# Delta-rule recurrence in chunks of 64 tokens, two pairs of sequences half a step apart, and mixed terms stored by whole heads

## What is computed

```python
q, k, v = (_short_conv(x @ W.T, conv) for W, conv in ...)      # 4 taps, silu
beta = sigmoid(x @ Wb.T)
# delta rule, chunk by chunk (the reference takes 32 tokens; any chunk gives the same result)
def step(S, inp):
    q_i, k_i, u_i, w_i = inp
    attn = jnp.where(causal, q_i @ jnp.swapaxes(k_i, -1, -2), 0.0)
    u_adj = u_i - w_i @ S
    o_i = q_i @ S + attn @ u_adj
    return (S + jnp.swapaxes(k_i, -1, -2) @ u_adj, o_i)
# u = T @ v, w = T @ (beta k), T the inverse of the chunk's unit lower triangle
o = p0 * fir3(v) + p1 * fir15(v) + p2 * fir63(v) + p3 * delta_out + p4 * v   # p: gates, softmax
x = layernorm(x + rmsnorm(o) @ Wo.T)
h = silu(x @ w1) * (x @ w2);  h = gelu(h @ h1);  h = gelu(h @ h2)
x = layernorm(x + h @ w3)
```

## Time and profile before

| what | before |
|---|---|
| median of 3 runs | 2404.92 us (2404.31 to 2409.49) |
| the profiled execution | 2403.26 us, span 2401.5 us |
| busy, of the span | PE 2159.4 us (90%), DVE 1209.4 (50%), ACT 926.3 (39%), POOL 521.5 (22%) |
| `delta` stage, first load to the next stage's first | 574.8 to 1067.1 us |
| one 128-token step in it | 28.0 us |
| DMA packets | 244243, of them 174162 under 512 B |
| mean granted TensorE clock | 0.962 of full speed |

### The profile page before, as it was taken

How to read it: one execution, slowest core, us unless ns; L and a number is a source line. 1 busy time by engine, 2 the same in 40 slices (tenths; PEclk the granted TensorE clock), 3 DMA queues, 4 the chain that set the end, 5 groups by cost and what they waited for, 6 DMA issues and landing times.

```text
span 2401.5 us, 40269 instructions
## 1 busy us (share of the span) xinstructions
PE 2159.4 (90%) x15412; PEld 1855.9 (77%) x15412; DVE 1209.4 (50%) x1877; ACT 926.3 (39%) x1556; POOL 521.5 (22%) x450
## 2 busy tenths in 40 slices
PE   7888864777899999949999999999999999999998
PEld 5776754666788888837888888888888888888886
DVE  6777759945676777742323432343244323323432
ACT  4554432011344444414433443444344434443442
POOL 1113787866344443410000000000000000000000
PEclk9999987788999999979999999999999999999999
DMA  3666667887899898823000000000000000000000
GB/s 125 195 196 180 198 180 216 265 291 217 210 244 249 237 243 225 221 102 160 1 18 18 17 0 17 17 17 0 17 17 16 2 17 17 0 17 17 18 1 18
DMA packets 244243, 253.36 MB, mean 106 GB/s; under 512 B 174162, under 2 KB 207442, under 8 KB 233810
## 3 DMA queue, kind: packets, MB, share of 16 engines
q1 hardware_dynamic: 231890, 210.54, 30.8%
q10 hardware_dynamic: 12288, 41.95, 5.3%
HBM read 156.77 MB, written 95.68 MB: 105 GB/s over the span
## 4 chain that ended last, share of the span: by engine, by line
PE 53%; issue 1%; DVE 1%; ACT 0%; DMA 0%; SPq 0%; POOL 0%; DVEq 0%; ACTq 0%; POOLq 0%
PE B L1671 47%; PE O L1699 5%; PE T L1627 1%; DVE yb L1798 0%; ACT gate L1737 0%; DMA wr<-wr_s 0%; SPq L1560 0%; DVE stats L1829 0%; ACT L1737 0%; DVE z L1824 0%; DVE z L1820 0%; DVE z L1843 0%; POOL rstd L1879 0%; SPq L1574 0%; DVEq L1793 0%
## 5 line engine op out<-in xcount | busy, mean ns | idle before, releaser
L1751 ACT ACTIVATE yb<-B,scol 128x512 f32<-128x512 f32 x256 | 176.2, 688 | 581.0 <-PE B L1671 581.0
L1671 PE MATMUL B<-act1l,wr 128*128 128x512 f32 x1024 | 398.4, 389 | 0.0
L1671 PE MATMUL B<-act0h,wr 128*128 128x512 f32 x1024 | 398.3, 389 | 0.0
L1671 PE MATMUL B<-act1h,wr 128*128 128x512 f32 x1024 | 398.3, 389 | 0.0
L1671 PE MATMUL B<-act0l,wr 128*128 128x512 f32 x1024 | 398.3, 389 | 0.0
L1786 DVE TENSOR_TENSOR act0l<-yb,act0h 128x512 fp32r<-128x512 f32 x256 | 176.0, 688 | 377.9 <-ACT act0h L1754 375.7
L1876 POOL TENSOR_TENSOR rstd<-mv,ln_eps 128x4 f32<-128x4 f32 x16 | 3.2, 199 | 1308.9 <-DVE mv L1837 1308.9
L441 DVE SCALAR_TENSOR_TENSOR acc<-proj,taps,acc 128x512 f32<-128x512 f32 x288 | 214.3, 750 | 85.2 <-ACT acc L387 76.7
L1786 DVE TENSOR_TENSOR act1l<-yb,act1h 128x512 fp32r<-128x512 f32 x128 | 88.6, 692 | 295.5 <-ACT act1h L1754 295.5
L1671 PEld LDWEIGHTS B<-act1l,wr 128*128 128x128 f32 x1024 | 192.2, 188 | 39.9
L1671 PEld LDWEIGHTS B<-act0l,wr 128*128 128x128 f32 x1024 | 192.2, 188 | 39.9
(11 more groups left out here) (179 smaller groups left out, 3448.7 us busy)
## 6 DMA issues: line engine op xcount, KB each, us to landing
qk_s<-yT SPq DMA_DIRECT2D x16, 1024.0 KB, 6.2
kk_s<-kfull SPq DMA_DIRECT2D x16, 1024.0 KB, 6.4
qk<-qk_s SPq DMA_DIRECT2D x16, 1024.0 KB, 6.6
lt<-kk_s SPq DMA_DIRECT2D x15, 1024.0 KB, 5.2
wraw<-in_ffn_w ACTq DMA_DIRECT2D x16, 704.0 KB, 5.9
wr_s<-wround ACTq DMA_DIRECT2D x16, 704.0 KB, 9.4
toe<-in_toe_short ACTq DMA_DIRECT2D x32, 320.0 KB, 7.2
xt<-in_xt SPq DMA_DIRECT2D x16, 524.0 KB, 4.3
```

Of the source, the lines that this page charges most:

```text
L1671: last = nc.tensor.matmul(B[slot % 4][:, :], w, part, start=(k == 0 and i == 0), stop=(k == kts - 1 and i == len(parts) - 1))
L1751: last = nc.scalar.activation(dst, B[slot % 4][:, :], ACT.Gelu, scale=scol[:, slot:slot + 1])
```

## The change

`weights_fir` keeps `mixed` for a whole head (64 features, two buffers), stores 4 times 2 MB instead of 8 times 1 MB, and `mix_s` is laid out by whole heads. `pwT` moves into memory of `raw`. The order of matrices in `kfull` and in the tables goes by sequence.

`delta` is written anew. Its unit is a group v of 32: one pair of sequences (e = v % 2) in one 128-token stretch (t = v // 2). Iteration u of 33 works the first 64 tokens of group u on partitions 0 to 63 and the second 64 tokens of group u-1 on partitions 64 to 127. So both pairs of sequences are in each iteration, and the four 32 x 32 inverses are joined only to two 64 x 64 ones (rounds "first" and "second" instead of N, A, B, C). Matmuls are on 64 x 64 quarters of the array, or on 128 x 64 halves, except the turn and the output projection. Loads have four buffers (`RING`), and one load of a kind serves half of what it did.

```diff
-C_ID, C_ATT, C_SEL, C_END = 0, P, 2 * P, 2 * P + 2
+C_ID, C_ATT, C_SEL, C_END = 0, P, P + P // 2, P + P // 2 + 2
+HC = 2 * CH
+GB = BATCH // 2
+GK = GB * KT
+GS = 2 * GK
+GROUPS = 2 * STEPS
+RING = 4
+WCH = W_END // GROUPS
 (weights_fir)
-        mixed = [st.sb(f"mixed{i}", [P, WIN, DK // 2]) for i in range(2)]
+        mixed = [st.sb(f"mixed{i}", [P, WIN, DK]) for i in range(2)]
-                    sp.wait_ge(mixed_done, (u + 1) * HALF)
+                    sp.wait_ge(mixed_done, (h + 1) * NG)
-                    if n > HALF // 2 and n % (HALF // PER_TOE) == 2:
-                        store(n // (HALF // PER_TOE) - 1)
+                    if h and g == 2:
+                        store(h - 1)
 (delta, tiles)
+        XY = st.ps("XY", [P, GK, 2, DK])
+        XO = st.ps("XO", [P, GK, 2, DK])
+        SI = st.ps("SI", [P, 2, 512])
+        Q = st.ps("Q", [P, 2, 512])
+        NA = st.ps("NA", [P, 2, GS, CH])
+        TW = st.ps("TW", [P, 512])
 (delta, SP: ten loads, two or four more, x, one store)
+                def group_in(v, r, n):
+                    sp.dma_start(qk[r][:, :, :], ...).then_inc(prep_in[p], 16)
+                    sp.dma_start(ktok[r][:, :, :], ...).then_inc(prep_in[p], 16)
+                    mats = bass.ds(t * NS + e * GS, GS)
+                    for c in range(2):
+                        j, i = FIRST[c], SECOND[c]
+                        sp.dma_start(lt[p][j, :, CH:HC], io["kk_s"][j, mats, i])
+                        sp.dma_start(tt[r][j, :, 0:CH], io["t_s"][mats, 2 * c].rearrange("s i j -> i s j"))
+                        sp.dma_start(tt[r][i, :, CH:HC], io["t_s"][mats, 2 * c + 1].rearrange("s i j -> i s j"))
+                        sp.dma_start(first_inv[p][j, :, :], io["d_s"][mats, 2 * c].rearrange("s i j -> i s j"))
+                def slot_in(part, r, p, t, e):
+                    rows = slice(part * HC, part * HC + HC)
+                    sp.dma_start(vtok[r][rows, :, :, :], ...)
+                    sp.dma_start(mix[r][rows, :, :, :],
+                                 io["mix_s"][part, bass.ds(t, 1), e * GB:(e + 1) * GB, :, :, :].rearrange("o b h m d -> m (o b) h d"))
+                def step(u, r, n):
+                    sp.wait_ge(s_ready, u + 1)
+                    sp.wait_ge(mixed, u)
+                    sp.wait_ge(prep_done, u + 2)
...
+                        group_in(u + 3, (r + 3) % RING, n + 2 if r % 2 else n + 1)
+                        slot_in(0, (r + 3) % RING, (r + 3) % 2, n + 2 if r % 2 else n + 1, (r + 3) % 2)
+                        slot_in(1, (r + 3) % RING, (r + 3) % 2, n + 1, r % 2)
+                        sp.wait_ge(res_done, u + 1)
+                        x_load(u - 1, (r - 1) % RING, n if r % 2 else n - 1)
+                        store(u - 3, (r + 1) % RING, n - 1 if r % 2 else n - 2)
 (delta, PE)
+                def from_state(u, r):
+                    pe.wait_ge(state_done, u)
+                    pe.wait_ge(u_done, u)
+                    for k in range(GK):
+                        for g, half, rows in chunks(u, r):
+                            last = nc.tensor.matmul(XY[rows, k, :, :], qk[g][:, KT + k % KT, tokens(k, half)], S[:, g % 2, k, :, :],
+                def queries_keys(v, r, n):
+                    for k in range(GK):
+                        for half in range(2):
+                            for par in range(2):
...
+                def first_round(v, r):
+                    for c in range(GS):
+                        for rows in HALVES:
+                            last = nc.tensor.matmul(NA[rows, 0, c, :], lt[r % 2][rows, c, :], first_inv[r % 2][rows, c, :],
+                def solve(u, r):
+                    pe.wait_ge(x_done, u + 1)
+                    for k in range(GK):
+                        for par in range(2):
+                            for g, half, rows in chunks(u, r):
+                                last = nc.tensor.matmul(XY[rows, k, par, :], tt[g][rows, par * GK + k, :], x0[rows, k, par, :],
+                def turn(u, r):
+                    pe.wait_ge(on_done, u + 1)
+                    pe.wait_ge(res_done, u + 2)
+                    for k in range(GK):
+                        last = nc.tensor.transpose(turned[:, k, :], o[r % 2][:, k, :, :].rearrange("p r d -> p (r d)"), ident)
+                def step(u, r, n):
+                    from_state(u, r)
+                    queries_keys(u + 1, ...)
+                    first_round(u + 1, ...)
+                    solve(u, r)
+                    queries_state(u, r)
+                    turn(u - 1, ...)
+                    new_state(u, r, n)
+                    queries_solution(u, r)
+                    second_round(u + 1, ...)
+                    project_out(u - 2, ...)
 (delta, ACT)
+                def step(u, r, n):
+                    first_out(u + 1, ...)
+                    solution(u, r)
+                    turned_out(u - 1, ...)
+                    second_out(u + 1, ...)
+                    squares(u, r)
+                    round_weights(u, r, n)
+                    raw_weights(u + 1, ...)
 (delta, DVE)
+                def step(u, r, n):
+                    right_side(u, r)
+                    head_norm(u - 1, ...)
+                    residual(u - 3, ...)
+                    causal(u + 1, ...)
+                    spread(u - 3, ...)
+                    state_out(u)
+                    outputs(u, r)
+                    compare_weights(u - 1, ...)
+                    head_sums(u)
+                    layer_norm(u - 3, ...)
 (delta, POOL)
+                def step(u, r, n):
+                    prep(u + 1, ...)
+                    tail(u - 3, ...)
+                    norm(u, ...)
-    "mix_s": (2, STEPS, BATCH, 2 * HEADS, WIN, DK // 2),
+    "mix_s": (2, STEPS, BATCH, HEADS, WIN, DK),
```

More of the change, by code:

```diff
@@ new lines, in delta, with rows_of, steps @@
+        NPREP = 10
+        LAST = GROUPS
+        def rows_of(u):
+            return slice(0, HC) if isinstance(u, int) and u == 0 else slice(HC, P) if isinstance(u, int) and u == LAST else slice(0, P)
+        def steps(engine, step, first, end):
+            loops = (end - first) // RING
+            with engine.Fori(0, loops) as i:
+                for j in range(RING):
+                    step(i * RING + (first + j), (first + j) % RING, i * (RING // 2) + (first + j) // 2)
+            return first + loops * RING
@@ L1008, in _ @@
+                for v in range(GROUPS - 3, GROUPS):
+                    store(v, v % RING, v // 2)
                 sp.wait_ge(flag_done, 1)
@@ new lines, in _ @@
+                queries_keys(0, 0, 0)
+                first_round(0, 0)
+                second_round(0, 0)
+                pe.wait_ge(ready, 4)
+                for u in range(3):
+                    if u == 2:
+                        pe.wait_ge(wo_done, 1)
+                    step(u, u % RING, u // 2)
+                u = steps(pe, step, 3, GROUPS)
+                while u <= LAST:
+                    step(u, u % RING, u // 2)
+                    u += 1
+                turn(LAST, LAST % RING)
@@ new lines, in _ @@
+                last.then_inc(tables_done, 1)
+                raw_weights(0, 0)
+                raw_weights(1, 1)
+                act.wait_ge(ready, 2)
+                first_out(0, 0)
+                second_out(0, 0)
+                for u in range(3):
+                    step(u, u % RING, u // 2)
+                u = steps(act, step, 3, GROUPS)
+                while u <= LAST:
+                    step(u, u % RING, u // 2)
+                    u += 1
+                turned_out(LAST, LAST % RING)
```

947 lines of the change are left out of this document (416 added, 531 removed).

## The result

The kernel after the change ran at 2367.05, 2370.82, 2372.29 and 2375.07 us, median 2371.56; the kernel before, beside it, at 2405.22. The ratio is 0.9856, with a 95% interval of 0.9835 to 0.9876. The change gains 33.7 us where the forecast expected 98. The profiled execution took 2375.07 us, its span 2373.2.

A forecast was written before the change was run, and what follows sets the result against it. The prediction took PE's queue to bound the kernel, with transfers not far behind. Replacing old `delta` and filter time by 24 + 32 x 11.2 - 3 + 20 gave 1949 + 32P = 2307 us, range 2272 to 2355.

The forecast's parts named there:

- The sum's form: Whole kernel: old time less old `delta` and 3 us of filters, plus beginning, 32 periods and end: 1949 + 32P.
- Filters: `weights_fir`: 6 us gained from POOL's vanished wait, 3 us lost on the 2 MB last store; net -3, between -9 and +4.
- PE's groups: `delta` loop: PE's matmul groups, transposes, projection and changes of array division take 10.7 us per iteration.
- the loop through the norms: `delta`: dependency loop from comparison through POOL's power, head norm, residual, statistics and state to outputs, 10.1 us together.
- row tiles don't queue: `solve`, `queries_solution`: alternating row tiles share a PSUM bank without queueing; the queueing rival gave P = 12.8, 2359 us, chance 0.03.
- DVE has room: `delta` loop: DVE needs 9.7 us per iteration including waits, leaving 1 us to spare.
- the period: `delta`: time per loop iteration, 11.2 us from PE's 10.7 and half a us of loss; ends 10.2 and 12.5.
- 16 x 0.68 = 10.9 us, or 16 x 0.56 = 9.0: `delta` loop: SP's time for its 16 transfer issues per iteration, the lower figure if nothing stalls.
- Transfers or SP bound the loop: Rival for the `delta` loop: P = 12 to 13.8, say 12.5, giving 2349 us, with PE idle before `queries_keys`; chance 0.13.
- In-order queues so close together don't interlock without loss: `delta` loop: reason for adding half a us of loss to PE's 10.7; PE lost 8% of a step before.
- what is late next are the Toeplitz loads: `weights_fir`: PE waits for these loads once POOL's wait goes, so 6 us of gain was counted, where 8.4 reached DVE.
- The wrong-if line: `delta` loop: the forecast is wrong if PE idles over 1 us per iteration, as the period is then not PE's.

The follow-up runs named there:

- e13: e4 with the two inverse rounds in PE's loop doing one of eight matrices, the rest left out (720 pairs in the body): 2292.28 us, one run, period 10.34.
- e1: Kernel after the change with PE's loop written out as 29 iterations, no jump back: 2366.91 us, ratio 0.9840.
- e4: Kernel after the change with the two loads of mixed terms issued by ACT instead of SP, which keeps 14 issues: 2354.84 us, ratio 0.9775.
- e6: e4 with PE's loop also written out: 2327.54 us, ratio 0.9664.
- e8: Kernel after the change with each head's mixed terms in the FIR stage stored as two 1 MB transfers instead of one of 2 MB: 2361.85 us, ratio 0.9824.
- e11: Kernel before the change with only PE's loop altered: four steps in its body instead of two, three times round: 2441.77 us, ratio 1.0148.
- e18: Against e15: PE's loop of four iterations kept, state and key products merged into larger matmuls (816 pairs in the body): 2373.25 us, ratio 0.9866.
- e15: Kernel after the change plus PE's loop written out, four loads issued by ACT, residual waiting for the store four groups ago, 1 MB FIR stores: 2308.53 us, ratio 0.9601.
- e17: Kernel after the change, all 16 issues on SP, inverse rounds in PE's loop doing one of eight matrices, the rest left out: 2346.68 us, ratio 0.9755.

## Why the prediction was wrong, point by point

- **The sum's form** held. Loop 413.8 us against 32 x 11.2 - 3 = 355.4, +58.4. First solve 20.6 us into the stage, forecast 24: -3.4. From the last one to `ffn` 23.8, forecast 20: +3.8. Filters +6.3, forecast -3: +9.3. Together +68.1, and 2307 + 68 = 2375, the profiled run.
- **PE's groups** were priced at 10.7 us (the terms as given add up to 10.6), and a quiet iteration takes 10.1. That is partly luck. `queries_keys` and `new_state` take 0.52 us each from their start to the next group's, not 0.95, because their matmuls start half as far apart as the earlier trace rows had them. Against that stands a wait of 0.5 us of `turn` for the residual, which has no term: `head_norm` waits 0.9 us for POOL just ahead of it, so the loop through the norms has little room, as forecast. The 64 x 64 groups of `solve` and `queries_solution` last 1.14 and 1.11 us; row tiles don't queue, as the earlier trace rows had it. DVE has room.
- **The step that failed is the period.** "I take 11.2 us, PE's 10.7 and half a us of loss". It measured 12.96. One term in it is wrong and two are missing.
  - SP "16 x 0.68 = 10.9 us, or 16 x 0.56 = 9.0": it measures 0.80 per issue, 12.7 us. The 0.68 came from twelve issues ahead of two long ones, in a loop in which SP waited 98 us in 320 for PE; in a queue that never waits the issues are longer. The rival "Transfers or SP bound the loop" had this mechanism at 0.13, and its 12 to 13.8 us hold the period measured, but it looked for the idle time in the wrong place: it shows at the residual and `turn`, through the store that SP issues last, not before `queries_keys`.
  - PE's instructions had no term and no rival. The loop body grew from 752 pairs (two steps of 376) to 944, past what stays. The trace before had 6 instruction packets in the stretch, so the old body stayed, and a count of the matmuls shows the growth; that the limit lies between the two could not be read there.
  - The clock had no term in the loop. It was 1.00 before, and the forecast prices PE at that; with the stalls it is 0.88, some 3 us at the jump shown above.
- "In-order queues so close together don't interlock without loss" is not what cost the time: with 14 issues and a body that stays (e13, with less work on PE) the quiet period is 10.1 us, iteration after iteration. e1 (A without the jumps, 12.68) and e4 (B with 14 issues, 12.50) each fall short of 12.96 us a little, both cures together far (e6, 11.53); the two losses mostly hide each other.
- **weights_fir**: POOL's wait for `mix_s` went, as forecast, and "what is late next are the Toeplitz loads" was right as well, but they were late by more than the wait saved; e8 puts that down to the 2 MB stores. The last of them is uncovered for 6.7 us, from 574.4 to 581.1, where 4.4 us passed before from POOL's last addition to the next stage. In the kernels above with this stage unchanged it ends between 579.5 and 583.1 us, so of the +9.3 some 2 us either way are scatter.
- **The wrong-if line** ("if PE idles over 1 us per iteration") came true: PE is idle 58.5 of 320 us, 2.4 per iteration. The range ended at 2355; the time is 17 us beyond it.

## What to carry to other kernels

Count what PE's loop body holds before it grows: here a body of 720 to 784 pairs of weight load and matmul ran without being fetched again (but for `ffn`'s 784 in e11), and one of 816 or more lost mostly 4 to 9 us at each jump back under traffic, and a stretch of full clock with it. Write such a loop out or jump seldom, and look whether the straight code still waits for "issue". Fewer matmuls are no gain if each then lasts longer (e18). Price a queue's issues at its own pace without rests (0.73 to 0.80 us here), not at that of a loop in which it waits, and count each small transfer. When one fix gives nothing, look at which wait grew, and try the second fix with it: 5 and -10 us alone were 48 together.

## What was not expected of the hardware

- PE's instructions come as packets of 16 KB among those of the same 16 transfer engines as the data (1.4% of their time): a refetched jump costs 1.7 to 2.1 us beside idle transfers and mostly 4 to 9 beside busy ones.
- Code that runs straight on, 29 iterations of 236 pairs, costs 8 us of waiting in 320 where the transfer engines are busy for 0.78 (e1), and 22 us where they are for 0.96 (e15); a body that stays costs under 2 (e13, e17).
- Records of 64 x 64 matmuls that go round all four quarters of the array into two PSUM banks (L1068, L1120) start 15.4 ns apart; those that alternate between two quarters in one bank (L1100) 29.8 ns. Whether the quarters or the banks make the difference was not tried.
- SP's issue of a 32 KB load (`lt`, `tt`) takes 0.33 us at rest and in the mean 0.44 to 0.68 in a queue that never waits.
- The transfers of this loop reach 276 GB/s on two queues, though most of their packets are under 512 B.
